# Three shifted row sums of a depthwise convolution added on GpSimd instead of accumulated by TensorE, for groups 5 to 7 of a mixed convolution, attention and expert kernel

## The reference, cut to what matters

```
x = x + conv_block(groupnorm(x))                  # the change is in here
t = tokens(x)                                     # 32*256 tokens of 64 channels
t = t + attention_block(layernorm(t))             # hashed buckets, 8 heads, then an MLP
t = t + expert_ffn(layernorm(t))                  # 8 experts, 2 picked for each token
```

```
out[h, w] = x[h, w] + xn[h, w] + bias + sum over dy, dx in 0..2 of xn[h + dy - 1, w + dx - 1]
```

## Time and profile before

| | |
|---|---|
| Median of 3 runs | 767.5 us |
| Profiled execution, its own time | 771.0 us |
| Its span, first to last instruction | 769.1 us |
| TensorE busy | 633.8 us (82%) |
| VectorE busy | 479.8 us (62%) |
| GpSimd busy | 369.3 us (48%) |
| ScalarE busy | 364.0 us (47%) |
| Mean granted TensorE clock | 0.897 |

### The profile page before, as it was taken

The page is one execution under the profiler, slowest core; times in us unless marked ns, Lnnn a source line. Parts: engine busy times, 40 slices in busy tenths (PEclk is TensorE's granted clock), DMA queues, the critical chain, the costliest instruction groups (busy, mean ns, idle before and its releaser), DMA issues.

```text
span 769.1 us, 14151 instructions
## 1 busy us (share of the span) xinstructions
PE 633.8 (82%) x4582; PEld 474.5 (62%) x4582; DVE 479.8 (62%) x1206; ACT 364.0 (47%) x710; POOL 369.3 (48%) x378
## 2 busy tenths in 40 slices
PE   2497889798559798889999999978978989999950
PEld 1476768667346675658657776756566657777730
DVE  2337677778408775578767877586756535555535
ACT  1133636465426364555557555654554435555520
POOL 2202250776702727764874558444755724444450
PEclk9658887879559899999999999999997989999985
DMA  2000000011132313352341416051542655555509
GB/s 85 5 15 1 15 0 15 18 46 60 35 121 83 124 37 111 117 146 90 107 149 54 160 60 187 18 158 37 183 130 63 188 159 165 161 164 161 165 6 327
DMA packets 46617, 75.50 MB, mean 98 GB/s; under 512 B 7488, under 2 KB 30048, under 8 KB 46544
## 3 DMA queue, kind: packets, MB, share of 16 engines
q1 hardware_dynamic: 35600, 57.67, 25.2%
q0 software_dynamic: 8640, 12.74, 4.8%
q10 hardware_dynamic: 2304, 4.20, 1.4%
HBM read 58.56 MB, written 16.47 MB: 98 GB/s over the span
## 4 chain that ended last, share of the span: by engine, by line
PE 42%; issue 17%; POOL 16%; DVE 15%; ACT 4%; DMA 4%; SPq 2%; POOLq 0%; ACTq 0%; DVEq 0%
PE bk L876 15%; POOL expert_rows L538 9%; PE bk L889 9%; DVE units L1558 3%; PE bk L786 3%; PE bk L660 2%; PE bk L831 2%; PE bk L751 2%; PE bk L725 2%; POOL rr L493 2%; POOL expert_results L546 2%; PE bk L896 1%; PE bk L776 1%; POOL r L499 1%; PE bk L681 1%
## 5 line engine op out<-in xcount | busy, mean ns | idle before, releaser
L876 PE MATMUL bk<-xs,wbuf 64*128 64x256 f32 x1704 | 209.9, 390 | 9.7 <-DVE units L1558 6.1
L546 POOL DMA_INDIRECT expert_results<-yout,xin x142 | 140.8, 992 | 144.8 <-DVE yout L1569 112.7
L1558 DVE TENSOR_TENSOR units<-bk,silu 128x512 f32<-128x512 f32 x213 | 143.9, 689 | 89.1 <-ACT silu L1135 88.5
L876 PEld LDWEIGHTS bk<-xs,wbuf 64*128 64x128 f32 x1704 | 161.6, 189 | 55.0 <-issue 27.0
L1135 ACT ACTIVATE silu<-bk 128x512 f32<-128x512 f32 x213 | 125.1, 596 | 84.9 <-PE bk L876 84.5
L538 POOL DMA_INDIRECT expert_rows<-srow,pos x128 | 130.7, 1021 | 70.7 <-issue 36.0
L889 PE MATMUL bk<-units,wbuf 128*64 128x256 f32 x852 | 108.9, 391 | 3.9 <-DVE ysum L1565 3.5
L889 PEld LDWEIGHTS bk<-units,wbuf 128*64 128x64 f32 x852 | 55.5, 137 | 39.8 <-issue 11.8
L1129 ACT ACTIVATE ysb<-bk 128x256 f32<-128x256 f32 x71 | 27.3, 384 | 86.0 <-PE bk L889 86.0
L493 POOL TENSOR_TENSOR rr<-vare,c_mhalf 128x16 f32<-128x16 f32 x8 | 23.5, 2937 | 83.1 <-DVE vare L1338 83.1
L831 PE MATMUL bk<-const,xin 128*128 128x128 f32 x142 | 30.0, 304 | 22.2 <-DMA xin<-expert_rows 15.1
(11 more groups left out here) (192 smaller groups left out, 979.8 us busy)
## 6 DMA issues: line engine op xcount, KB each, us to landing
wbuf<-in_weights SPq DMA_DIRECT2D x71, 576.0 KB, 4.0
xin<-expert_rows SPq DMA_DIRECT2D x71, 130.0 KB, 3.4
expert_results<-yout,xin POOLq DMA_INDIRECT x142, 3.1
xg<-in_x SPq DMA_DIRECT2D x8, 256.0 KB, 2.8
expert_rows<-srow,pos POOLq DMA_INDIRECT x128, 2.4
srow<-expert_results SPq DMA_DIRECT2D x8, 256.0 KB, 5.3
srow<-expert_results ACTq DMA_DIRECT2D x8, 256.0 KB, 6.3
out<-hid ACTq DMA_DIRECT2D x8, 256.0 KB, 5.6
```

Source lines behind the costliest of these rows:

```text
L546: g.indirect_dma_start(results[:, :], bass.IndirectOffsetOnAxis(ap=xin[:, t % X_SLOTS, h, ROW - 1:ROW].bitcast(U32), axis=0), yout[:, t % ...
L876: last = mm(bank[:, ch * MT:(ch + 1) * MT], wbuf[part, t % W_SLOTS, at:at + P], xs[part, t % 2, :], start=True, stop=True)
L1558: tt(units[:, t % 2, q, :], h3_ps[q], silu[:, q, :], ALU.mult).then_inc(unit_ready, 1)
```

## The change

For groups 5 to 7 (`a >= MIX`) GpSimd gets a new step `line_sums(a)`. It waits for `hsum` and `xres` of the group and adds the three row shifts of `hsum` to `xres`, in place, one after the other, each waiting for the one before. It stands in the first burst at k = 2, behind the scatter of the results of the burst's first tile. TensorE then waits for the third addition and turns each block of `xres` with one plain turn: 4 turns a group in place of 4 + 12 products. Groups 0 to 4 stay as they are.

```diff
+        line_step = sem("line_step")
...
+            def line_sums(a):
+                pool.wait_ge(conv_ready, a + 1)
+                pool.wait_ge(xres_ready, 2 * a + 2)
+                for dy in range(3):
+                    wait(pool, line_step, 3 * (a - MIX) + dy)
+                    g.tensor_tensor(xres[:, :, :, :], xres[:, :, :, :], hsum[:, :, dy:dy + HH, :], ALU.add)\
+                        .then_inc(line_step, 1)
+
...
+                    if k == 2:
+                        run(a, line_sums)
                     if k == 3 and i > MIX:
                         run(b, unit_sum)
...
                 if a >= MIX:
                     pe.wait_ge(ysum_ready, 2 * BURSTS[a, 0][1] - 2)
+                    pe.wait_ge(line_step, 3 * (a - MIX) + 3)
                 for f in range(2):
                     o = t_ps[:, (2 * s + f) * P:(2 * s + f + 1) * P]
                     h0 = f * HH // 2
+                    if a >= MIX:
+                        last = turn(o, xres[:, s, h0:h0 + 8, :].rearrange("p h w -> p (h w)"), ident)
+                        continue
                     mm(o, xres[:, s, h0:h0 + 8, :], ident, start=True, stop=False)
```

## The result

The changed kernel takes 777.02 us (median of 4 runs, 776.67 to 778.95), the kernel before 768.33 us beside it (4 runs, 766.65 to 769.26). The ratio is 1.0119, with a 95% interval of [1.0099, 1.014]: slower by 8.7 us, where the forecast was 2.8 us. The changed kernel's profiled execution took 777.33 us with a span of 775.5 us, so between the two profiles there are 6.3 us. The rest of the 8.7 us is that the profiled execution of before was a long one: it lay 2.7 us above its median, that of the changed kernel 0.3 us. The two kernels were profiled once more later, at 770.05 and 778.44 us, 8.4 us apart; of these, 1.6 us arise ahead of the first instruction that the change touches. From the first expert tile to the last, the first pair of profiles is 6.6 us apart and the second 7.0 us.

What follows compares the result with a forecast made beforehand. It took VectorE's own queue to bound the attention of iterations 6 and 7, and TensorE at the slow clock that of iteration 5. Gains 3.8, losses 6.6, net +2.8 us on 767.5: 770.3 us, range 764.0 to 773.0.

Steps and rivals of the forecast that it cites:

- Gain of iteration 5: Attention stage: without the slow-clock products, VectorE's waits for scores 3 and before the reciprocal shrink; together 2.8 us.
- The rival premise, that the slow clock lasts: Iteration 5: less TensorE work to bring the clock back, gain only 0.3 us, net +5.3 us, 772.8 us; 12%.
- the bound of 0.3 us: Iteration 5's attention: lower bound of the gain, 0.3 us, if the slow clock lasts through attend 1.
- Gain of iterations 6 and 7: Attention stages: VectorE's own queue is late next, so TensorE's saving yields only 0.5 us each, 1.0 us for both.
- Iteration 8 as the model of a stage without a convolution: Iteration 8's attention takes 9.91 us against iteration 6's 10.45 us, so the convolution's removal gains 0.5 us.
- Hold of iteration 5: GpSimd's second addition holds VectorE's L1569, delaying the sum, schedule and scores TensorE waits for: +0.7 us.
- Iteration 6: Hold in schedule_tiles: three additions each hold one small VectorE operation, the gate comes later: +3.5 us.
- Iteration 7: Hold: L1537, L1540 and L1546 meet one addition each, so the gate starts at 428.3: +2.4 us.
- GpSimd's own 12 us and TensorE's wait: Groups 5 to 7: additions of 4.0 us a group fit idle time, sums are ready before TensorE needs them: nothing.
- The sum: Whole kernel: gains 3.8 us, losses 6.6 us, net +2.8 us, giving 770.3 us.
- The rival by recorded starts: Holds begin only at the addition's recorded start; VectorE slips past the third: 3.8 against 3.9, 767.5 us; 22%.
- The step that failed: Iteration 6, first burst: TensorE's last up product waits for VectorE's held gate, so the +3.5 us is passed on whole.

Runs made afterwards that it cites:

- e9: Kernel before, with the second half of TensorE's convolution moved behind attend 0 in the mixed iterations; 769.14 us, ratio 0.9995.
- e1: Changed kernel, but GpSimd's three additions write a tile of their own and TensorE keeps its products; 780.0 us, ratio 1.0131.
- e3: Changed kernel with three GpSimd memsets of a tile of its own in place of the additions; 768.66 us, ratio 0.999.
- e2: Changed kernel with the plain turns alone: GpSimd adds nothing, TensorE doesn't wait, row sums left out; 768.21 us, ratio 0.9978.
- e7: Kernel before, with five (iteration 6) and four (iteration 7) VectorE reductions ahead of schedule_tiles, nothing new on GpSimd; 776.77 us, ratio 1.009.
- e8: e4 with the second half of TensorE's convolution moved behind attend 0 in the mixed iterations; 769.45 us, ratio 1.0005.
- e4: The change for group 5 alone, groups 6 and 7 as in the kernel before; 768.51 us, ratio 0.9982.
- e5: Changed kernel with the additions of groups 6 and 7 one step later, behind unit_sum, past schedule_tiles; 769.32 us, ratio 1.0001.
- e6: The change for groups 6 and 7 alone, group 5 as in the kernel before; 779.09 us, ratio 1.0122.

## Why the prediction was wrong in size

The sign was right, with 2.8 us forecast and 6.3 us between the profiles, 8.7 us between the medians.

- **Gain of iteration 5** (2.8 predicted): 2.40. Against the second profile of before it is 2.1. The rival premise, that the slow clock lasts, came true: the window of 266 is at 0.50, where it was back at 1.00. Its price didn't follow. The two waits shrank by 2.5 us even at the slow clock, so the bound of 0.3 us was set too low.
- **Gain of iterations 6 and 7** (0.5 each): 0.42 and 0.41. Iteration 8 as the model of a stage without a convolution held, and e9 agrees with its reason.
- **Hold of iteration 5** (0.7): 0.57. **Iteration 6** (3.5): 3.42. **Iteration 7** (2.4): 2.40, though the first operation held was L1551 (L1536 before) and not L1537 as named; the end of the third addition sets the size, whichever operation comes first. e1 gives the same values without the turns, e2 none of them.
- **GpSimd's own 12 us and TensorE's wait** (nothing): at most 0.5 us, by e3 against e2.
- **The sum.** The terms that the prediction had come to 6.39 - 3.23 = +3.2 us, against 2.8. The rival by recorded starts (3.8 us of holds) is out: the holds reach ahead of the recorded start in iteration 6.

That the terms come so near the forecast is no luck in the holds, which e1 repeats. What is missing is a term for TensorE's clock. The step that failed is the one that passed a hold on one for one: "TensorE's last up product of the burst waits for that gate, so nothing hides it". It is true and not enough. That wait leaves TensorE idle, and the clock falls behind it; the sum priced everything after iteration 5 at the full clock. The changed kernel lost 1.26 us there in iteration 6, and this part is shown: e1 lost 1.12 us without the turns, and e7 1.13 us with VectorE late for another reason. It lost 1.15 us in iteration 7, where e1 and e7 with the same idle time lost nothing. The third place, iteration 8's 2.33 us, was foreseen by nothing in the prediction. Together the slow clock took 4.74 us, while 1.10 us came back in iteration 9 for a cause that is open. Rows 5 had shown what such a fall costs, and I had it as a rival for iteration 5 only.

**What stays open.** In iteration 7 the clock fell only where both the hold and the turns of group 6 were there; why the turns count isn't shown. What decides the fall in iteration 8, where the idle time and the products are the same in all thirteen profiles, isn't settled. It goes with the turns of group 7: all six profiles that have them fell, and of the seven without them only e8 did. But those turns stand some 70 us earlier, and e8 fell with its products kept, so this is an association and no cause. The holds don't decide it: e1 and e7 have them and didn't fall, e2 hasn't and did. So 1.15 and 2.33 us of the profiled 6.3 are located, and not derived. With one profile for most kernels, an execution's own share isn't told apart from the kernel's: the twelve executions of e4 go from 764.57 us at a mean granted clock of 0.898 to 772.5 us at 0.888. Filling TensorE's idle time with other work, which would test the clock's part directly, was not tried.

## What to carry to other kernels

Work on GpSimd that reads SBUF is free for GpSimd and dear for VectorE, by its place: the same additions cost 3.4 us beside a row of small VectorE operations and 0.3 us one step later (e5). So look for a stretch in which VectorE reads from PSUM or waits. And where a change makes another engine late in a burst, price TensorE's clock behind the new idle time as well as the delay, as a range from nothing up: here it was 1.12 to 2.57 us on top of the delay in iteration 6 in every kernel with it, and in iteration 7 1.15 to 1.19 us in some and nothing in others.

## What was unexpected of the hardware

- A TENSOR_SCALAR of 128 x 8 float32 was held beside an addition (L1551, 1.09 us for 0.22, which reads a column of `const` too) and beside a memset (L1562, one input, 1.02 us for 0.17), while operations with two SBUF inputs passed the memset at 0.16 us.
- The held L1555 is recorded from 0.36 us ahead of the addition (339.86 and 340.22), at 1.70 us, and again at 1.70 us in the second execution.
- TensorE's clock fell at different moments behind its idle time. In the changed kernel the eight products next behind 3.74 us of it took 1.13 us, at full clock, and those after them were slow; in e1, e6 and e7 the same eight, behind 4.60, 3.57 and 3.09 us, took 2.08, 2.08 and 1.95 us.
- Two kernels with the same idle time of 2.37 and 2.38 us ahead of the same twelve products got different clocks there (1.52 and 2.06 us).
